# Feed-forward with its narrowing blocks in groups of four and a 32-column spread, finished by GpSimd behind the turned queries

## The reference

```python
    def _L1_ffn_ref(x, c_fc_1, c_fc_2, c_proj_1, c_proj_2):
        w_fc = jnp.kron(c_fc_1, c_fc_2)        # (1536 x 32) kron (1 x 12)
        w_proj = jnp.kron(c_proj_1, c_proj_2)  # (32 x 1536) kron (12 x 1)
        h = x @ w_fc.T
        h = jax.nn.gelu(h, approximate=False)
        out = h @ w_proj.T
        return out
...
    t = t + _L1_ffn_ref(_ln_t(t), L1_ffn_c_fc_1, L1_ffn_c_fc_2, L1_ffn_c_proj_1, L1_ffn_c_proj_2)
```

## Time and profile before

| | |
|---|---|
| median of 3 executions | 3124.77 us (3123.82 to 3130.79) |
| the profiled execution | 3126.24 us |
| its span in the profile | 3124.5 us |
| TensorE busy | 2768.5 us, 89% of the span |
| VectorE, ScalarE, GpSimd busy | 2187.7, 1763.3 and 1767.5 us |
| mean granted TensorE clock | 0.963 of full speed |

### The profile page before, as it was taken

The page is one execution under the profiler, slowest core; times in us unless marked ns, Lnnn a source line. Parts: engine busy times, 40 slices in busy tenths (PEclk is TensorE's granted clock), DMA queues, the critical chain, the costliest instruction groups (busy, mean ns, idle before and its releaser), DMA issues.

```text
span 3124.5 us, 68549 instructions
## 1 busy us (share of the span) xinstructions
PE 2768.5 (89%) x29084; PEld 1590.4 (51%) x29084; DVE 2187.7 (70%) x3787; ACT 1763.3 (56%) x2090; POOL 1767.5 (57%) x1166
## 2 busy tenths in 40 slices
PE   1689998999889999899988999989999899889997
PEld 1346563565536554365634556346563565535553
DVE  2476776768768686786857867677776768757684
ACT  2456555566555665565645656556556565555563
POOL 6457373664546656374653737457374574647563
PEclk9799999999999999999999999999999999999998
DMA  2000001000010000100001000100001000010000
GB/s 94 21 21 2 1 2 42 22 2 1 2 62 2 2 2 1 62 2 1 2 11 52 2 1 2 41 22 2 1 2 42 22 2 1 2 42 2 2 2 21
DMA packets 32751, 48.11 MB, mean 15 GB/s; under 512 B 5152, under 2 KB 32032, under 8 KB 32448
## 3 DMA queue, kind: packets, MB, share of 16 engines
q1 hardware_dynamic: 29904, 41.55, 4.0%
q10 hardware_dynamic: 2544, 2.18, 0.2%
HBM read 30.95 MB, written 12.58 MB: 14 GB/s over the span
## 4 chain that ended last, share of the span: by engine, by line
PE 47%; POOL 15%; DVE 15%; issue 12%; ACT 6%; POOLq 0%; DVEq 0%; ACTq 0%
PE ps L486 11%; POOL pl L926 8%; PE ps L812 7%; POOL ph L969 5%; PE ps L602 5%; DVE mxp L882 4%; PE ps L773 4%; PE ps L782 4%; PE ps L737 4%; DVE pl L926 3%; PE ps L1235 3%; PE ps L775 2%; DVE x L1042 2%; DVE stats L1046 2%; PE ps L1253 2%
## 5 line engine op out<-in xcount | busy, mean ns | idle before, releaser
L926 POOL TENSOR_TENSOR pl<-p,ph 128x1024 f16<-128x1024 f32 x336 | 825.2, 2456 | 402.4 <-ACT ph L859 387.4
L882 DVE TENSOR_REDUCE mxp<-ps 128x1 f32<-128x512 f32 (+2 forms) x1344 | 777.8, 626 | 188.7 <-PE ps L737 181.3
L857 ACT ACTIVATE p<-ps 128x1024 f32<-128x1024 f32 (+1 forms) x672 | 644.8, 961 | 450.8 <-PE ps L782 444.6
L812 PEld LDWEIGHTS ps<-v,ph 128*128 128x128 f16 x9600 | 516.6, 98 | 129.5 <-issue 37.6
L926 DVE TENSOR_TENSOR pl<-p,ph 128x1024 f16<-128x1024 f32 (+1 forms) x336 | 414.8, 1234 | 214.4 <-POOL ph L969 212.3
L812 PE MATMUL ps<-v,ph 128*128 128x65 f16 (+1 forms) x9600 | 540.6, 195 | 20.4 <-DVE pl L926 12.5
L812 PE MATMUL ps<-v,pl 128*128 128x65 f16 x4800 | 517.8, 194 | 0.0
L812 PEld LDWEIGHTS ps<-v,pl 128*128 128x128 f16 x4800 | 452.0, 100 | 0.0
L617 POOL TENSOR_TENSOR v<-o,v 128x384 f16<-128x384 f32 x128 | 113.5, 891 | 517.9 <-ACT o L613 517.7
L782 PE MATMUL ps<-qc,kc 65*128 65x512 f16 (+3 forms) x1344 | 388.1, 371 | 0.0
L859 ACT ACTIVATE ph<-p 128x1024 f16<-128x1024 f32 x336 | 355.6, 1058 | 10.7
(11 more groups left out here) (182 smaller groups left out, 5300.7 us busy)
## 6 DMA issues: line engine op xcount, KB each, us to landing
x<-in_x SPq DMA_DIRECT2D x8, 1536.0 KB, 7.8
out<-x SPq DMA_DIRECT2D x16, 768.0 KB, 3.8
xin<-in_x SPq DMA_DIRECT2D x7, 1536.0 KB, 6.8
xin<-in_x ACTq DMA_DIRECT2D x1, 1536.0 KB, 19.8
qc<-rowt SPq DMA_DIRECT2D x96, 2.0 KB
o<-in_L_conv_qkv_w SPq DMA_DIRECT2D x2, 576.0 KB, 11.4
p<-in_L_conv_qkv_w SPq DMA_DIRECT2D x1, 576.0 KB, 13.0
x<-in_L_attn_Wq SPq DMA_DIRECT2D x1, 576.0 KB, 13.0
```

The source lines that it names most:

```text
L812: mm = nc.tensor.matmul(m.ps[:, 6 + half % 2, c0:c0 + w], e, v, start=(first and n == 0), stop=(g in self.last_of_half and n == len(work) ...
L857: nc.scalar.activation(m.p32[:, i % RING, :, 0:w], m.ps[:, 2 * (i % 2):2 * (i % 2) + 2, 0:w], ACT.Exp, scale=SCALE).then_inc(s["exp"], 1)
L882: nc.vector.reduce_max(m.mxp[:, h % 2, kh, qt:qt + 1], m.ps[:, bank, 0:w], AX.X).then_inc(s["free"], 1)
L926: engine.tensor_tensor(m.pl[:, i % RING, :, 0:w], m.p32[:, i % RING, :, 0:w], m.ph[:, i % RING, :, 0:w], ALU.subtract).then_inc(sem, 1)
```

## The change

Six things are changed together.

1. Narrowing: `down(n)`, n from 0 to 5, issues the four blocks of two gelus together, one for each strip, instead of two and two. It stands behind `up` and the filling products at i = 2n + 2.
2. Spread: the constant matrix is 32 columns wide (it only adds the four strips), without c_proj_2. Four tiles are issued together, `spread(0)` at i = 8 and `spread(1)` behind the last `down`, into one bank each (6 and 0).
3. `widen(n)`, new, on VectorE: for two tiles at once it multiplies the 32 sums from PSUM with the 12 numbers of c_proj_2 into 768 f32 numbers per partition, in ring slots 2 and 3 of `ph` or `pl`. `widen(2)` and `widen(3)` wait until GpSimd has used the buffers of `widen(0)` and `widen(1)`.
4. `add(n)`, for two tiles, moves from VectorE to GpSimd, behind the 12 instructions of `turn`.
5. TensorE waits for `widened` 2 ahead of `v_products(0)` and for `widened` 4 ahead of `rel_products(1)`, instead of for all adds.
6. The preparation makes a 32-column constant and no longer multiplies it.

```diff
-            for j in range(4):
-                sv = m.spread[j * FA:(j + 1) * FA, :].rearrange("p (a b) -> p a b", b=FB)
-                carve(sv, ALU.not_equal, 1.0, 0, [[-1, FA], [0, FB]], 1)
+                carve(m.spread[j * FA:(j + 1) * FA, :], ALU.not_equal, 1.0, 0, [[-1, FA]], 1)
...
-    def down(self, pe, i):
+    def down(self, pe, n):
-        hf, f = i // self.PAIRS, 2 * (i % self.PAIRS)
-        pe.wait_ge(s["act"], s.at("act", i + 1))
-        for j in range(2):
-            q = (f + j) % 4
-            mm = self.nc.tensor.matmul(m.ps[q * FA:(q + 1) * FA, 6 + hf, :], m.cp[:, f + j, :], m.p32[:, i % self.NHID, j, :],
-                                       start=(f + j < 4), stop=(f + j >= NF - 4), skip_group_check=True)
+        hf, f = 2 * n // self.PAIRS, 4 * n % NF
+        pe.wait_ge(s["act"], s.at("act", 2 * n + 2))
+        for q in range(4):
+            mm = self.nc.tensor.matmul(m.ps[q * FA:(q + 1) * FA, 6 + hf, :], m.cp[:, f + q, :], m.p32[:, (2 * n + q // 2) % self.NHID, q % 2, :],
+                                       start=(f == 0), stop=(f == NF - 4), skip_group_check=True)
...
-        self.nc.tensor.matmul(self.m.ps[:, self.BANKS[t], 0:C], self.o2[:, t * P:(t + 1) * P], self.m.spread[:, :], start=True, stop=True).then_inc(self.s["spread"], 1)
+        for t in range(4 * hf, 4 * hf + 4):
+            mm = self.nc.tensor.matmul(self.m.ps[:, self.BANKS[hf], t % 4 * FA:(t % 4 + 1) * FA], self.o2[:, t * P:(t + 1) * P], self.m.spread[:, :], start=True, stop=True)
+        mm.then_inc(self.s["spread"], 1)
...
-        self.nc.vector.tensor_tensor(self.m.x[:, t, :], self.m.ps[:, self.BANKS[t], 0:C], self.m.x[:, t, :], ALU.add).then_inc(self.s["added"], 1)
+    def widen(self, dve, n):
+        hf, t = n // 2, 2 * (n % 2)
+        dve.wait_ge(self.s["spread"], self.s.at("spread", hf + 1))
+        if hf == 1:
+            dve.wait_ge(self.s["added"], self.s.at("added", 2 * (n - 1)))
+        y = self.m.ps[:, self.BANKS[hf], t * FA:(t + 2) * FA].rearrange("p (t a) -> p t a", a=FA)
+        self.nc.vector.tensor_tensor(self.widened(n), y.unsqueeze(3).broadcast_to([P, 2, FA, FB]),
+                                     self.m.cp2[:, :].unsqueeze(1).unsqueeze(1).broadcast_to([P, 2, FA, FB]), ALU.mult).then_inc(self.s["widened"], 1)
+    def add(self, pool, n):
+        pool.wait_ge(self.s["widened"], self.s.at("widened", n + 1))
+        x = self.m.x[:, 2 * n:2 * n + 2, :]
+        self.nc.gpsimd.tensor_tensor(x, self.widened(n).rearrange("p t a b -> p t (a b)"), x, ALU.add).then_inc(self.s["added"], 2)
...
+                if before and t == 0:
+                    pe.wait_ge(before.ff.s["widened"], before.ff.s.at("widened", 2))
...
-                        pe.wait_ge(before.ff.s["added"], before.ff.s.at("added", NT))
+                        pe.wait_ge(before.ff.s["widened"], before.ff.s.at("widened", 4))
...
-                if i >= 1:
-                    ff.down(pe, i - 1)
                 if i < 2 * ff.PAIRS and FILL[i] and w.next:
                     after.fill(pe, 3 * EACH + sum(FILL[:i]), 3 * EACH + sum(FILL[:i + 1]))
-                if i in SPREADS:
-                    ff.spread(pe, SPREADS.index(i))
-            for t in range(4, NT):
-                ff.spread(pe, t)
+                if i >= 2 and i % 2 == 0:
+                    ff.down(pe, i // 2 - 1)
+                if i == 8:
+                    ff.spread(pe, 0)
+            ff.spread(pe, 1)
```

More of the change, by code:

```diff
@@ L85, in allocate @@
     m.cp2 = sb("cp2", [P, FB], F32)
-    m.spread = sb("spread", [P, C], F32)
+    m.spread = sb("spread", [P, FA], F32)
     m.group = sb("group", [P, NC_, C], F32)
@@ L215, in _ @@
             nc.vector.tensor_tensor(m.bv16[IMG:IMG + 1, :], m.bv[IMG:IMG + 1, :], m.bv16[IMG:IMG + 1, :], ALU.subtract)
-            nc.vector.tensor_tensor(m.spread[:, :].rearrange("p (a b) -> p a b", b=FB), m.spread[:, :].rearrange("p (a b) -> p a b", b=FB),
-                                    m.cp2[:, :].unsqueeze(1).broadcast_to([P, FA, FB]), ALU.mult)
         @block.gpsimd
@@ L1140 @@
     PAIRS = NF // 2
-    BANKS = (6, 6, 6, 6, 0, 1, 0, 1)
-    COUNTS = dict(scaled=8, summed=8, offset=2, x2=8, x2_t=2, x2_hi=4, x2_lo=2, up=12, act=12, each=12, o2=2, spread=8, added=8)
+    BANKS = (6, 0)
+    COUNTS = dict(scaled=8, summed=8, offset=2, x2=8, x2_t=2, x2_hi=4, x2_lo=2, up=12, act=12, each=6, o2=2, spread=2, widened=4, added=8)
     def __init__(self, nc, m, s, proj):
@@ L1237, in down @@
         mm.then_inc(s["each"], 1)
     def o2_out(self, dve, hf):
[L1240 removed]
+        dve.wait_ge(self.s["each"], self.s.at("each", self.PAIRS // 2 * (hf + 1)))
         self.nc.vector.tensor_copy(self.o2[:, hf * BANK:(hf + 1) * BANK], self.m.ps[:, 6 + hf, :]).then_inc(self.s["o2"], 1)
[L1243 to L1253 removed]
@@ L1255, in add, with spread @@
-    def add(self, dve, t):
-        dve.wait_ge(self.s["spread"], self.s.at("spread", t + 1))
-        self.nc.vector.tensor_tensor(self.m.x[:, t, :], self.m.ps[:, self.BANKS[t], 0:C], self.m.x[:, t, :], ALU.add).then_inc(self.s["added"], 1)
+    def spread(self, pe, hf):
+        pe.wait_ge(self.s["o2"], self.s.at("o2", hf + 1))
+        if hf == 1:
+            pe.wait_ge(self.s["act"], self.s.at("act", 2 * self.PAIRS))
+        for t in range(4 * hf, 4 * hf + 4):
+            mm = self.nc.tensor.matmul(self.m.ps[:, self.BANKS[hf], t % 4 * FA:(t % 4 + 1) * FA], self.o2[:, t * P:(t + 1) * P], self.m.spread[:, :], start=True, stop=True)
+        mm.then_inc(self.s["spread"], 1)
@@ new lines, in widened @@
+    def widened(self, n):
+        buf = self.m.ph if n % 2 == 0 else self.m.pl
+        return flat(buf[:, 2:4, :, :].rearrange("p r a b -> p r (a b)")).bitcast(F32)[:, 0:2 * C].rearrange("p (t a b) -> p t a b", t=2, b=FB)
+    def widen(self, dve, n):
+        hf, t = n // 2, 2 * (n % 2)
+        dve.wait_ge(self.s["spread"], self.s.at("spread", hf + 1))
+        if hf == 1:
+            dve.wait_ge(self.s["added"], self.s.at("added", 2 * (n - 1)))
+        y = self.m.ps[:, self.BANKS[hf], t * FA:(t + 2) * FA].rearrange("p (t a) -> p t a", a=FA)
+        self.nc.vector.tensor_tensor(self.widened(n), y.unsqueeze(3).broadcast_to([P, 2, FA, FB]),
+                                     self.m.cp2[:, :].unsqueeze(1).unsqueeze(1).broadcast_to([P, 2, FA, FB]), ALU.mult).then_inc(self.s["widened"], 1)
@@ L1438, in vector @@
             ff.o2_out(dve, 0)
-            for t in range(4):
-                ff.add(dve, t)
-                if t in (1, 2):
-                    low(4, (t - 1,))
+            low(4, (0,))
+            ff.widen(dve, 0)
+            ff.widen(dve, 1)
+            low(4, (1,))
             low(5, (0,))
             ff.o2_out(dve, 1)
-            ff.add(dve, 4)
-            ff.add(dve, 5)
             low(5, (1,))
-            ff.add(dve, 6)
-            ff.add(dve, 7)
+            ff.widen(dve, 2)
+            ff.widen(dve, 3)
         def gpsimd(pool, w):
@@ L1469, in gpsimd @@
                     w.next.qkv0.turn(pool, n)
+            for n in range(4):
+                ff.add(pool, n)
         def sync(sp, b, w):
```

13 lines of the change are left out of this document (2 added, 11 removed).

## The result

The changed kernel takes **3080.8 us**, median of four runs (3077.2 to 3082.7), where the kernel before took 3127.7 beside it (3123.8 to 3130.8): ratio 0.985, 95% interval 0.983 to 0.987, some 47 us less. Forecast were 3071 with 3058 to 3102. The profiled execution took 3079.4 us. The forecast took 53.4 us off a median of 3124.8 that was known then; with the further execution beside the changed kernel that median is 3127.7. So of the 10 us between 3071 and 3080.8 some 3 are the starting point, and 6.5 are what the change gave less than forecast (46.9 for 53.4).

The account below looks back on a forecast made before the run. TensorE was taken to bound the boundaries. Per boundary 5.9 + 3.8 less some 2.0 of waits gives 7.7; 7 x (7.7 - 0.5) + 3.0 = 53.4 us off the median 3124.8: 3071 us, range 3058 to 3102.

Parts of the forecast that it names:

- Groups of four at 0.98: Narrowing on TensorE: four strips cost what two cost, 0.98 us; six groups replace twelve pairs, 5.9 us less per boundary.
- The rivals of pairs and of serial strips: Narrowing: four strips take as long as two pairs, 3108 us, chance 0.10; or run one after another, 3190 us, chance 0.03.
- Spread at 0.22 per matmul, 0.9 for four: Spread matmuls of 32 columns on TensorE: 0.22 us each, 0.9 for four; 3.8 us less per boundary.
- the rule that the prediction named from the Trainium skill: Spread: about 60 cycles per matmul however narrow, 0.05 us each; 1.4 us more gain per boundary, left out of the sum.
- Waits given back, `v_products(0)` at 31.3: Boundary on TensorE: some 2.0 us of new waits, `v_products(0)` at 31.3 instead of 39.0; 7.7 us less per boundary.
- `rel_products(1)` hidden by 0.2 us: Position products: `widen(3)` ends at 35.9, `rel_products(1)` is due at 36.1, so its wait stays hidden.
- ScalarE's cover: Position products: ScalarE, slower in taking out products, would hide much of a `rel_products(1)` 1.2 us late.
- The allowance of 0.5 a boundary: Small losses from late `rel_low` and `rel_products(1)`: 0.5 us per boundary, with bounds of 0 and 1.5.
- `turn` doesn't move: GpSimd: `turn` still ends at 31.2 from the first `up`, since its start hangs on queries of i = 0 and 1.
- Half clock, "all seven alike": Boundaries: half clock behind the table load in three of seven makes the gain no smaller; all seven counted alike.
- the rival of the clock: Clock falls in new TensorE idle time ahead of position products: some +30 us, 3101 us; chance 0.12 for most boundaries.
- Preparation, 3.0 less: Before TensorE's first matmul: smaller GpSimd selects save about 2.4 us, a dropped VectorE multiplication 0.6; 3.0 us less.
- The last image, 0: Last image: smaller `down` and spread offset by 3.8 us of widens and serial adds behind the last spread; 0 in total.

Follow-up runs that it names:

- Experiment 5: Changed kernel with `widen(2)` and `widen(3)` writing into free buffers of their own, so they wait for no add: 3069.5 us, ratio 0.981.
- experiment 6: Changed kernel with `v_products(0)` of the next image issued ahead of the last narrowing group, in the wait for the last gelu: 3065.4 us, ratio 0.979.
- experiment 2: Changed kernel with `down` back in pairs, keeping the narrow spread and the rest: 3106.8 us, ratio 0.992.
- experiment 9: Changed kernel with ScalarE's last gelu ahead of the `pair_high` between the last two, and VectorE's copy ahead of one `pair_low`: 3075.6 us, ratio 0.982.
- experiment 8: Changed kernel with all four adds on VectorE behind the widens, instead of on GpSimd behind `turn`: 3094.7 us, ratio 0.989.
- 10: Changed kernel with own widen buffers, early `v_products(0)`, and the turned order (last gelu ahead of `pair_high`, copy ahead of `pair_low`): 3084.6 us, ratio 0.983.
- 1: Kernel before with only `down` in fours; spread, copies and adds unchanged: 3085.5 us, ratio 0.987.
- 3: Changed kernel with each group of four blocks on two strips: 3104.4 us, ratio 0.992.
- 4: Changed kernel with each group of four blocks on one strip: 3188.4 us, ratio 1.018.
- 7: Changed kernel with both own buffers for `widen(2)` and `widen(3)` and `v_products(0)` ahead of the last group: 3053.0 us, ratio 0.975.

## Why the prediction was right, and what in it was not

- **Groups of four at 0.98**: measured 1.00, and two and one strip show why (1.85, 3.55). The rivals of pairs and of serial strips fall. This term and the next carry the result, and they were right by mechanism and size.
- **Spread at 0.22 per matmul, 0.9 for four**: measured 0.92. With 32 columns in place of 384 the time is no longer that of the columns. The row of one-column matmuls was the right neighbour. By the rule that the prediction named from the Trainium skill, TensorEngine Tiling (Array Packing), Instruction Overhead, it would have been 0.05 each, and the trace does not agree.
- **Waits given back, `v_products(0)` at 31.3**: measured 30.7 in clean boundaries; the gain is 8.3, not 7.7. The wait for the last gelu is 1.43, forecast 1.6. The term that was too big is the pace between the groups: two i and a group take 4.57 us (1226.72 to 1231.29), where the sum had 4.68. `up` costs the 0.54 us of the earlier trace rows where a `down` follows it, but 0.44 where a fill does (1241.32 to 1241.76), and in the stretch that the prediction read a `down` stood behind each of them.
- **`rel_products(1)` hidden by 0.2 us**: wrong. Due 4.79 behind `v_products(0)` and thus at 35.5, it came at 36.1 (0.53 us of wait in its row; the last `widen` ends at 36.0), where the forecast put the end of `widen(3)` well enough (35.9). So the step that failed is the due time, for the same reason as above: TensorE came 0.6 us earlier than forecast to a wait that didn't move. Experiment 5 prices it at 1.0 us at the first scores of a clean boundary; ScalarE's cover, which I counted on, hid nothing there. The allowance of 0.5 a boundary was half of that, but only two boundaries of the profiled execution have the wait.
- **`turn` doesn't move**: right, 31.25 to 31.4. GpSimd's add at 1.8: 1.81. Widen at 1.0: 0.95.
- **Half clock, "all seven alike"**: the weakest step. Behind the table load it falls in three of seven boundaries, as before, but in three boundaries the clock falls behind the last group too, where the kernel before had none in its trace (its nearest begins 13 us behind `v_products(0)`). The clean boundaries say 64.4 us to the first scores and the three took 71.7, 66.9 and 66.6; not all of these 12 us is the new place. The 17.1 us at half clock that begin there are 8.6 us of lost clock. That is the rival of the clock, in single boundaries as the range had it; experiment 6, with one such fall, has 13 us less up to the first scores. The boundaries gave 54.4 for 50.4 even so, since a clean one gives 8.2 us at the first scores where the sum had 7.2: the pace was a little better than forecast, and behind `v_products(0)` only 0.1 of the 0.5 is lost against the kernel before.
- **Preparation, 3.0 less**: the selects went from 3.36 to 1.26 us and the first query product came 2.45 us earlier. But the first `up` of the first boundary came 1.8 later than before. At TensorE's first row of `ps<-ident,o` 2.4 us of the gain were still there (232.3 for 234.7); at its first row of `ps<-wo_hi,hT` there was a loss of 2.9 (313.5 for 310.6). Two stretches at half clock begin in between, at 237.5 and 247.7, where the kernel before has one, at 288.4; the changed kernel has one at 292.1 too. So what was saved did not reach the end.
- **The last image, 0**: 35.18 and 35.19. The last spread starts 2.06 us earlier (25.44 for 27.50 behind the first `up`), and from it to the end takes 9.75 us for 7.68, with the widens, the two serial adds and the store. That both are equal is luck in part: the changed kernel's last image has 14.7 us at half clock and the one before 8.3.

Taken together: boundaries -54.4 (forecast -50.4), preparation and first image +1.8 (-3.0), rest of the images +5.6 (0), last image 0. So the 6.5 us that the change gave less than forecast lie wholly outside the boundaries: 4.8 ahead of the first one and 5.6 in the images between, less the 4.0 that the boundaries gave more. The forecast came near because errors of opposite sign met. **What stays open** is what decides whether the clock falls at one place. In the profiled executions it fell behind the last group in 3 of 7 boundaries of the changed kernel, in 1 of experiment 2 (in two more it falls 11 us behind `v_products(0)`), in 4 of experiment 9, in 1 of experiment 6, in all of 8 and 10, and in none of 1, 3, 4, 5 and 7. Idle time there goes with it: it is longest in 8 and 10, and filled in 6 and 7. But experiment 5 has the changed kernel's idle time and none of the falls, and experiment 9 has four of them with 1.11 and 0.81 us of idle time, where experiments 1, 3 and 4 have the same or nearly the same and none. So the idle time alone does not decide. The +5.6 us in the attention were not taken apart either; the image with the most half clock there is the longest (304.5 us with 17.1 at half clock) and the one with the least the shortest of the full ones (301.9 with 10.2), but between them the order isn't strict, and in sum the half clock there is 100 us for 101 before. So more of it is not the reason.

## What to carry to other kernels

When a step on the bounding engine gets shorter, recount the due time of every instruction behind it with the shorter time: a wait that was hidden by 0.2 us is a wait, and its buffer was the cheapest thing to fix (1 us in a clean boundary, for two buffers that lay free). Put work that is ready into the wait ahead of a burst on TensorE: in the clean boundaries it brought next to nothing, and with fewer falls of the clock some 12 us in the profiled execution. And two parts of a change should be compared at a point in the trace too, where here they added up to 0.01 us, and not only by the medians, where they missed by 20: the difference says where to look.

## What was unexpected of the hardware

- Four full-height strips of 32 columns take 1.00 us for four f32 matmuls of 512 columns, two strips 1.85, one 3.55, nearly in inverse proportion to the number of strips. A group of four costs what the pair in the earlier trace rows costs (0.98).
- An f32 matmul of 32 columns with full weights takes 0.23 us, as one of one column does (0.22 to 0.24). The loads of the weights are busy for nearly as long; that they set the pace fits this, but no run tested it. In the last image of the changed kernel the weight loads of four (PEld) are busy for 0.97 us, the matmuls for 1.08.

```profile
3067.86 0.97 PEld L1244 LDWEIGHTS ps<-spread,pl 128*128 128x128 f32 x8 [1.72 <-DVE pl L1236]
3067.86 1.08 PE L1244 MATMUL ps<-spread,pl 128*128 128x32 f32 x8 [0.81 <-DVE pl L1236]
```

- A two-input f32 add of 768 numbers per partition, all in SBUF, takes 1.81 us on GpSimd, 0.95 on VectorE alone, and 1.71 to 2.67 on VectorE beside GpSimd's `turn` (all seven boundaries of experiment 8), where two of the six `turn` instructions take 2.5 us instead of 1.9.
